# First layer of a graph network: one product of 144 columns per tile and bucket instead of three of 48, into three banks in turn

## What is computed

```
x = _layernorm(x + _L0_gnn_ref(x, edge_weight1, ..., src, dst, edge_type_8))    # relations
x = _layernorm(x + _L1_gnn_ref(x, edge_weight1, src, dst))                     # softmax over edges
x = _layernorm(x + _L2_gnn_ref(src, dst, x))                                   # two propagations
x = _layernorm(x + _L3_gnn_ref(x, edge_index, edge_attr_40, ...))              # gated messages
```

```
h1 = relu(einsum('ni,rij->nrj', inputs, weight1) + bias1)
h2 = einsum('nrj,rjo->nro', h1, weight2)
msg = h2[src, rel_type] * norm
agg = segment_sum(msg, dst, num_segments=6250)
return relu(agg + bias2)
```

## Time and profile before

| | us |
|---|---|
| runs shown, median of 3 | 6890.07 (6889.62 to 6891.36) |
| the profiled execution's own time | 6896.36 |
| its span | 6894.1 |
| first layer, first to last L2229 | 232.5 to 2764.1 |
| PE busy | 3935.5 (57%) |
| DVE busy | 4076.4 (59%) |
| POOL busy | 3949.5 (57%) |
| ACT busy | 2562.1 (37%) |

### The profile page before, as it was taken

The page is one execution under the profiler, slowest core; times in us unless marked ns, Lnnn a source line. Parts: engine busy times, 40 slices in busy tenths (PEclk is TensorE's granted clock), DMA queues, the critical chain, the costliest instruction groups (busy, mean ns, idle before and its releaser), DMA issues.

```text
span 6894.1 us, 121916 instructions
## 1 busy us (share of the span) xinstructions
PE 3935.5 (57%) x46612; PEld 3010.7 (44%) x46613; DVE 4076.4 (59%) x7184; ACT 2562.1 (37%) x5259; POOL 3949.5 (57%) x3993
## 2 busy tenths in 40 slices
PE   6455555545545554355555555556555565887775
PEld 5344444323323323134444444444444444776774
DVE  4444444555555556345566666566666568667999
ACT  1111111111111111244455445445445445776664
POOL 2566666666666666655555555555555553225996
PEclk8555555555555555555555555555555555999998
DMA  3455422222222222133333233333333332667886
GB/s 128 166 159 165 122 48 47 49 53 48 48 47 48 48 48 46 30 52 55 56 57 59 54 57 55 56 57 57 55 58 56 55 57 53 190 186 172 193 191 132
DMA packets 1414672, 571.31 MB, mean 83 GB/s; under 512 B 1069539, under 2 KB 1353711, under 8 KB 1413953
## 3 DMA queue, kind: packets, MB, share of 16 engines
q1 hardware_dynamic: 1309185, 452.39, 29.4%
q0 software_dynamic: 104896, 110.96, 7.3%
HBM read 394.81 MB, written 168.16 MB: 82 GB/s over the span
## 4 chain that ended last, share of the span: by engine, by line
another core or an unknown queue 23%; PE 18%; issue 16%; ACT 16%; DVE 13%; DMA 9%; SPq 2%; POOL 1%; DVEq 0%; ACTq 0%; POOLq 0%
DMA rb<-dst_rows 6%; PE ps L1250 4%; ACT rb L1606 3%; ACT meta_b L1616 3%; DMA meta_b<-blocks 3%; DVE ps L2099 2%; ACT meta_a L1538 2%; PE ps L1288 2%; PE ps L1421 2%; ACT rb L1636 2%; ACT at_table L1636 2%; PE ps L1210 2%; ACT meta_b L1623 1%; PE ps L1238 1%
## 5 line engine op out<-in xcount | busy, mean ns | idle before, releaser
L928 POOL DMA_INDIRECT by_src<-meta_a,row_src x1612 | 1609.5, 998 | 1343.2 <-DVE meta_a L2354 922.6
L917 POOL DMA_INDIRECT ring<-h_table,meta_b x1616 | 1641.9, 1016 | 945.8 <-issue 452.7
L1523 ACT ACTIVATE ring<-ring,meta_b 128x48 f32<-128x48 f32 x1616 | 386.4, 322 | 2142.1 <-DMA ring<-h_table,meta_b 2104.3
L1421 PE MATMUL ps<-dst_i,meta_b 128*128 128x128 bf16 x2450 | 398.7, 295 | 901.5 <-ACT rb L1636 331.5
L1250 PE MATMUL ps<-ring,WX 128*128 128x48 bf16 x2188 | 440.2, 235 | 559.7 <-DVE row_src L2230 331.3
L2593 DVE TENSOR_TENSOR meta_b<-big,ps 128x1152 bf16<-128x1152 bf16 x546 | 734.5, 1346 | 0.0
L1421 PEld LDWEIGHTS ps<-dst_i,meta_b 128*128 128x128 bf16 x2450 | 229.6, 152 | 1133.1 <-issue 1107.3
L1250 PE MATMUL ps<-row_src,WX 128*128 128x48 bf16 x4376 | 502.5, 233 | 261.5 <-issue 260.1
L1380 PE MATMUL ps<-WX,meta_b 128*128 128x49 bf16 (+1 forms) x14742 | 591.4, 200 | 61.0 <-issue 28.2
L1250 PEld LDWEIGHTS ps<-ring,WX 128*128 128x128 bf16 x2188 | 358.7, 164 | 591.7 <-DVE row_src L2230 343.3
L1288 PE MATMUL ps<-meta_a,w1T 40*48 40x256 f32 x806 | 401.6, 596 | 358.6 <-DMA meta_a<-in_attrT 179.1
(11 more groups left out here) (343 smaller groups left out, 9058.7 us busy)
## 6 DMA issues: line engine op xcount, KB each, us to landing
meta_b<-blocks SPq DMA_DIRECT2D x490, 144.0 KB
by_src<-default SPq DMA_DIRECT2D x44, 1456.0 KB
meta_a<-by_src SPq DMA_DIRECT2D x273, 216.0 KB, 4.4
rb<-lo_rows SPq DMA_DIRECT2D x202, 256.0 KB
rb<-src_rows SPq DMA_DIRECT2D x273, 144.0 KB
rb<-dst_rows SPq DMA_DIRECT2D x273, 144.0 KB
meta_a<-in_attrT SPq DMA_DIRECT2D x402, 80.0 KB
ring<-h_table,meta_b POOLq DMA_INDIRECT x1616
```

The lines of the kernel that those rows point to most:

```text
L917: pool.indirect_dma_start(ring[:, gg % RING, j, 0:width], None, table, bass.IndirectOffsetOnAxis(ap=index(g * GROUP + j), axis=0)) \
L928: pool.indirect_dma_start(by_src, bass.IndirectOffsetOnAxis(ap=row_src[:, t:t + 1], axis=0), rec[:, q % RECS, j, :], None).then_inc(s_sc[q ...
L1421: mm = pe.matmul(bank(5, P, at=i * P), ohS_n[:, a % 3, :, u * TRIO + i], ohK_n[:, a % 2, u * TRIO + i, :], start=True, stop=True)
L1523: scaled = act.activation(row, row, ACT.Copy, scale=meta_b[:, t, M_NORM:M_NORM + 1])
```

## The change

The upper half of the product still comes from ACT, but ACT now writes it to a buffer of two slots instead of back into the ring, and the three parts of a row lie there side by side, 144 columns. The buffer is the tensor `X`. So:

- `sum_fixed`: one product of 144 columns per tile and bucket, into bank `b % 3`; the three parts are not yet added to each other. The first product of a bucket starts the sum, so nothing is zeroed. Ahead of the first product of bucket b >= 3, PE waits until bucket b-3 has been taken out (`s_taken`).
- `take_bucket` on DVE: one reduction over the three parts, from PSUM to `V[:, b, :]`, in the iteration after the bucket's last group.
- ACT waits, from group 2 on, for PE's sums of group g-2 (`s_used`). POOL waits for ACT's copy (`s_rown`) in place of PE's sums.
- `relations` becomes one addition on `V` and is a step of `first_norm`, which starts at place 4 of the second stage (before: place 0); ACT's square root for it goes from place 7 to 12.
- `X` is loaded with `x` after the last sum. The tile numbers are loaded again for `cell_tables`, at group 12, into another tensor (`scratch`); `place_cells` uses another scratch tensor.
- For the form that isn't run, buckets are summed and taken out as before with one more step (`sums_out`, `late_sums`).

```diff
+FIRST_OF = [next(t for t in range(TILES_IN) if FROM[t] + WIDE[t] > b) for b in range(N_BUCKETS)]
+LAST_OF = [max(t for t in range(TILES_IN) if FROM[t] <= b) for b in range(N_BUCKETS)]
+ROLLS = 3
+assert all(FIRST_OF[b + ROLLS] // GROUP > LAST_OF[b] // GROUP + 1 for b in range(N_BUCKETS - ROLLS))
...
-        parts_w = row_src[:, 0:4 * GROUP * FEAT].bitcast(F32).rearrange("p (s i j w) -> p s i j w", s=2, i=2, j=GROUP)
-        parts_h = row_src[:, 0:4 * GROUP * FEAT].bitcast(BF16) \
-            .rearrange("p (s i j w k) -> p s i j w k", s=2, i=2, j=GROUP, k=2)[:, :, :, :, :, 1]
-        ring_h = ring[:, :, :, :].bitcast(BF16)[:, :, :, 1:2 * FEAT:2]
+        parts_x = X[:, :, :].rearrange("p b w -> p (b w)")[:, 0:2 * GROUP * PARTS * FEAT]
+        parts_w = parts_x.rearrange("p (s j i w) -> p s j i w", s=2, j=GROUP, i=PARTS)
+        parts_h = parts_x.bitcast(BF16).rearrange("p (s j c k) -> p s j c k", s=2, j=GROUP, k=2)[:, :, :, :, 1]
...
# SP
-                if g == PLAN_AT + 20:
-                    sp.wait_ge(s_hit2, 1)
-                    sp.dma_start(X[:, :, :], A["x"]).then_inc(s_node, 16)
+                if g == TILE_NO_AT:
+                    sp.dma_start(tile_at, A["tile_no"][:, 0:TILES_IN]).then_inc(s_node, 16)
+
+            sp.wait_ge(s_used, 2 * GROUPS_IN)
+            sp.dma_start(X[:, :, :], A["x"]).then_inc(s_node, 16)
...
# POOL, gather
-                    if gg >= RING:
-                        pool.wait_ge(s_used, 2 * (gg - RING + 1))
-                        pool.wait_ge(s_adapt, min(gg - RING + 1, GROUPS_IN))
+                    old = gg - RING
+                    if 0 <= old < GROUPS_IN:
+                        pool.wait_ge(s_rown, old + 1)
+                        pool.wait_ge(s_adapt, old + 1)
...
# PE, sum_fixed
                     for h in range(WIDE[T]):
-                        for rows in (ring_h[:, g % RING, j, :], parts_h[:, g % 2, 0, j, :], parts_h[:, g % 2, 1, j, :]):
-                            mm = pe.matmul(acc_of(FROM[T] + h, FEAT), hot_w[:, g % 2, h, :, j], rows,
-                                           start=False, stop=False, skip_group_check=True)
+                        b = FROM[T] + h
+                        if T == FIRST_OF[b] and b >= ROLLS:
+                            pe.wait_ge(s_taken, TAKEN + b - ROLLS + 1)
+                        mm = pe.matmul(bank(b % ROLLS, PARTS * FEAT), hot_w[:, g % 2, h, :, j], parts_h[:, g % 2, j, :],
+                                       start=(T == FIRST_OF[b]), stop=(T == LAST_OF[b]))
...
# ACT
+                if g >= 2:
+                    act.wait_ge(s_used, 2 * (g - 1))
...
-                    t, row = g * GROUP + j, ring[:, g % RING, j, 0:FEAT]
-                    scaled = act.activation(row, row, ACT.Copy, scale=meta_b[:, t, M_NORM:M_NORM + 1])
+                    t = g * GROUP + j
+                    scaled = act.activation(parts_w[:, g % 2, j, 0, :], ring[:, g % RING, j, 0:FEAT], ACT.Copy, scale=meta_b[:, t, M_NORM:M_NORM + 1])
...
# DVE, fixed_group
-                link(dve.tensor_tensor(rest, rows, ring_h[:, g % RING, 0:n, :], ALU.subtract))
-                dve.tensor_tensor(low, rest, parts_h[:, g % 2, 0, 0:n, :], ALU.subtract).then_inc(s_w, 2)
+                link(dve.tensor_tensor(rest, rows, top[0], ALU.subtract))
+                dve.tensor_tensor(low, rest, top[1], ALU.subtract).then_inc(s_w, 2)
...
+            def take_bucket(b):
+
+                dve.wait_ge(s_used, 2 * (LAST_OF[b] // GROUP + 1))
+                dve.tensor_reduce(V[:, b, :], bank(b % ROLLS, PARTS * FEAT).rearrange("p (i w) -> p w i", i=PARTS), AX_X, ALU.add) \
+                    .then_inc(s_taken, 1)
...
# DVE, end of an iteration of first_layer, and relations
+                    if fixed:
+                        for b in range(N_BUCKETS):
+                            if LAST_OF[b] // GROUP == g - 1:
+                                take_bucket(b)
...
             def relations():
-
-                for k in range(ACC_BANKS):
-                    last = dve.tensor_tensor(banks(V)[:, k], acc[:, k, :, 0:FEAT],
-                                             rb2[:, None, :].to_broadcast([P, PER_BANK, FEAT]), ALU.add)
-                last.then_inc(s_epi, 1)
-                dve.wait_ge(s_epi, 2)
+                return dve.tensor_tensor(V[:, :, :], V[:, :, :], rb2[:, None, :].to_broadcast([P, SLOTS, FEAT]), ALU.add)
```

More of the change, by code:

```diff
@@ L463, in build @@
         assert COS_AT < GROUPS_IN
-        NORM_AT = 7
+        FIRST_NORM_AT = 4
+        NORM_AT = FIRST_NORM_AT + 8
+        TILE_NO_AT = 12
         FIELDS_LAG, TABLES_LAG, ROWS_LAG = 10, 13, 16
@@ L1180, in sum_quads @@
                         for h, regs in enumerate((here, after)):
+                            rows = parts_w[:, gg % 2, t, 0, :] if gg < GROUPS_IN else ring[:, gg % RING, t, 0:width]
                             mm = pe.matmul(ps[:, bass.ds(regs[t], width)], W[:, i, j, h * P:(h + 1) * P],
-                                           ring[:, gg % RING, t, 0:width], start=False, stop=False,
+                                           rows, start=False, stop=False,
                                            skip_group_check=True)
@@ L2111, in _ @@
             rows_f = VQ[:, 2 * TILES_IN:3 * TILES_IN]
-            tmp = [VQ[:, i * TILES_IN:(i + 1) * TILES_IN] for i in range(2)]
+            tmp = big[:, TILES_IN:2 * TILES_IN]
             def place_cells():
@@ L2218, in fixed_group @@
             def fixed_group(g):
-                n, t = len(tiles_of(g)), g * GROUP
-                rows = ring[:, g % RING, 0:n, 0:FEAT]
-                rest, low = parts_w[:, g % 2, 0, 0:n, :], parts_w[:, g % 2, 1, 0:n, :]
+                n = len(tiles_of(g))
+                rows, rest, low = [parts_w[:, g % 2, 0:n, i, :] for i in range(PARTS)]
+                top = [parts_h[:, g % 2, 0:n, i * FEAT:(i + 1) * FEAT] for i in range(2)]
                 if g == 0:
@@ L2228, in fixed_group, with sums_out, first_layer @@
                     dve.wait_ge(s_used, 2 * (g - 1))
-                link(dve.tensor_tensor(rest, rows, ring_h[:, g % RING, 0:n, :], ALU.subtract))
-                dve.tensor_tensor(low, rest, parts_h[:, g % 2, 0, 0:n, :], ALU.subtract).then_inc(s_w, 2)
+                link(dve.tensor_tensor(rest, rows, top[0], ALU.subtract))
+                dve.tensor_tensor(low, rest, top[1], ALU.subtract).then_inc(s_w, 2)
                 if g + 1 < GROUPS_IN:
                     place_hots(g + 1)
-            def first_layer(weights_of):
+            def take_bucket(b):
+                dve.wait_ge(s_used, 2 * (LAST_OF[b] // GROUP + 1))
+                dve.tensor_reduce(V[:, b, :], bank(b % ROLLS, PARTS * FEAT).rearrange("p (i w) -> p w i", i=PARTS), AX_X, ALU.add) \
+                    .then_inc(s_taken, 1)
+            def sums_out():
+                dve.wait_ge(s_used, 2 * GROUPS_IN)
+                for k in range(ACC_BANKS):
+                    last = dve.tensor_copy(banks(V)[:, k], acc[:, k, :, 0:FEAT])
+                return last
+            def first_layer(weights_of, fixed):
                 early = [split(src_i, lo_src, link)]
@@ L2267, in first_layer @@
                         steps(early, 3)
+                    if fixed:
+                        for b in range(N_BUCKETS):
+                            if LAST_OF[b] // GROUP == g - 1:
+                                take_bucket(b)
                 steps(early, 1000)
+                if fixed:
+                    for b in range(N_BUCKETS):
+                        if LAST_OF[b] // GROUP == GROUPS_IN - 1:
+                            take_bucket(b)
+                    dve.memset(V[:, N_BUCKETS:SLOTS, :], 0.0).then_inc(s_epi, 1)
+                else:
+                    sums_out().then_inc(s_epi, 1)
             dve.tensor_copy(place_8, iota_b[:, 0:P][:, :, None].to_broadcast([P, P, GROUP])).then_inc(s_place, 1)
@@ L2288, in _, with late_sums @@
             dve.tensor_scalar(far[:, 1:2], small[:, 6, 0:1], 0.5, None, ALU.is_le).then_inc(s_far, 1)
-            def relations():
-                for k in range(ACC_BANKS):
-                    last = dve.tensor_tensor(banks(V)[:, k], acc[:, k, :, 0:FEAT],
-                                             rb2[:, None, :].to_broadcast([P, PER_BANK, FEAT]), ALU.add)
-                last.then_inc(s_epi, 1)
-                dve.wait_ge(s_epi, 2)
+            def late_sums():
+                for k in range(ACC_BANKS):
+                    last = dve.tensor_tensor(banks(V)[:, k], acc[:, k, :, 0:FEAT], banks(V)[:, k], ALU.add)
+                last.then_inc(s_epi, 1)
+                dve.wait_ge(s_epi, 3)
+            def relations():
+                return dve.tensor_tensor(V[:, :, :], V[:, :, :], rb2[:, None, :].to_broadcast([P, SLOTS, FEAT]), ALU.add)
             def cell_tables_of(d):
```

57 lines of the change are left out of this document (35 added, 22 removed).

## The result

| | before | changed |
|---|---|---|
| median of the runs beside each other, us | 6889.84 (4 runs, 6878.81 to 6891.36) | 6975.5 (4 runs, 6958.09 to 7000.69) |
| ratio, 95% interval | | 1.0133 (1.0108 to 1.0157) |
| span of the profiled execution | 6894.1 | 6969.6 |
| time of a group in the first layer | 12.59 | 13.01 |
| from the last group's subtraction to the end | 4130.0 | 4121.1 |

A forecast was written before the change was run, and what follows sets the result against it. The first layer was taken to be bound by the ring between DVE and PE, with POOL's gathers as floor. Terms -138 - 163 + 15 - 3 = -289 us gave 6607, with the runs' median 6601 us; range 6460 to 6790 (0.82).

The forecast's parts named there:

- the ring between DVE and PE: First layer: DVE splits, PE sums and counts, DVE scans before the next split; taken to set 12.59 us a group.
- The sums, -138: PE's sums: one product of 144 columns for three of 48, 187 to 124 ns at 2188 places, 138 us less.
- The back-to-back rule: PE's products follow each other by N / 1.2 ns at the low clock, which would make the sums' gain 0.
- The breaks, -163: Unexplained idle time before PE's sums, 488.0 us; middle between 325 us less and nothing taken, 163 us less.
- POOL's release: POOL's ring slot is free without PE's sums, so gathers may start earlier; data already wait for DVE, counted as nothing.
- ACT's copy, 0: ACT scales into two slots and waits for PE's group before the last; 18.7 us cover its 1.9, cost 0.
- the slower rival: ACT starts only at PE's late post and DVE's split waits: 384 us more, less the 289, about 6985 us; chance 0.07.
- The rest, -3: Five additions before the second stage become one inside it, 3 us less; moved load and late norm 0 each.
- breaks stay: Rival: PE's unexplained idle time does not shrink, only -138 + 15 - 3 = -126 us, 6764 us; chance 0.19.
- nothing moves: Rival: gathers pace PE by themselves, a group stays at 12.59 us whatever PE does, 6887 us; chance 0.07.

The follow-up runs named there:

- after_third: The changed kernel unaltered, run again on a chip where the kernel before takes 5611.4 us: 5606.1 us, ratio 0.9986.
- three_used: The changed kernel with three products of 48 columns and POOL again waiting for PE's sums: 6837.7 us, 1.0085 of the kernel before.
- used: The changed kernel with POOL's gather again waiting also for PE's sums of the slot's last group: 6811.0 us, 1.0031 of the kernel before.
- the holds: Kernels in which POOL's gathers of group g wait for PE's sums of g-3 or g-2; in the changed kernel 0.9858 and 0.9836 of the kernel before.
- The hold of g-2: The changed kernel with POOL's gather of group g waiting for PE's sums of g-2: 6771.64 us, 0.9836 of the kernel before.
- the two holds: The changed kernel, a group's first four gathers waiting for PE's sums of g-3, the last four for g-2: 0.9987 and 0.999; 0.9841 on a slower chip.

## Why the prediction was wrong

- *What bounds the kernel.* "POOL is not the bound" and "the ring between DVE and PE" were right by their rows and yet missed the point: on these chips the ring is long because POOL gathers. Halving the gathers took 4.9 us off the group with the ring's own work unchanged, 4.8 of them off DVE's wait for PE. I had written that I do not know what starves PE and that it decides the case; the sum then went on with a middle value.
- *The sums, -138.* The term was right in size. Eight products of 144 columns take 1.18 us, so (1.18 - 0.32) / 7 = 0.123 us each, where 0.124 was taken. PE's busy time from 200 to 1150 us fell from 462 to 369 us. As time it was worth 27 to 37 us under the old release. The back-to-back rule that I set against it ("TensorE: Matmul & The Clock Gate" of the Trainium skill, Back-to-back issue gap) gives 0.120 us for 144 columns, near the 0.123 measured; it is at 48 columns that the trace has 62 ns and the rule 40.
- *The breaks, -163.* This step failed. I took the middle between "goes with the count" and "goes with time", and it does not go with the count: 684.6 us of "issue" before PE's products became 634.1, and over all its products 753 became 779. It goes with the gathers (149 us with half of them) and with the chip (none before products in `after_third`). The statement that fetching is hidden ("Runtime: NRT & Kernel Launch" of the Trainium skill, Instruction fetch mechanics), which I had let speak for a rival only, fits this far: fewer instructions gave nothing of their own beyond the products' time.
- *POOL's release, "I count nothing".* This step failed too, and it is the largest cost: 0.7 to 1.0% with one product and 3.4% with three. I priced what the earlier start could bring, and not what the gathers that start earlier do to PE.
- *ACT's copy, 0.* This failed by size. DVE waited 15.0 us for it (10.8 before), so the slower rival that I had named (ACT as a link of the ring, 384 us) did not happen at its place. But ACT waits 2024 us for PE or "remote", and passes the lateness of PE's posts on to POOL, whose new release it is (243.8 us). Copy, wait and taking out together cost 46 to 58 us in `three_used`, of which I had 15, and 14 are the reductions. DVE's wait for ACT grew by 8 to 21 us; the rest, some 10 to 35 us, I cannot place. This cost and the product's gain nearly cancel, and with the release on top the sign turned.
- *The rest, -3.* It was -9.
- The forecast's sum was 289 us less, and the measured one is 86 more. Of the rivals, "breaks stay" had the breaks right, and "nothing moves" had PE paced by the gathers but not the loss; none had the release.

What stays open: why PE's posts are late while POOL gathers on some chips and not on others. The traces show the delay, that it goes with the number of gathers or of their rows, and that a post is prompt in a pause of POOL and mostly late outside one; they do not show the thing that is shared. Rows and gathers were not told apart. That the release costs is shown on one chip with three products, and with one product only across chips, as the change was not run beside `used`. How it costs is in part argued: DVE's wait for PE falls when the release is given back, with the holds and with half the gathers, but neither the mean lag of the sums' posts nor the share of double bursts, by which I meant to show it, orders the times. ACT's wait for PE was not taken out by itself. The hold of g-2 in the changed kernel was not run on a chip of 5610 us; the two holds were, at 0.999.

## What to carry to other kernels

If hand-overs between two engines are late while a third issues gathers, treat that third engine's start times as a cost: a wait that looks superfluous may be what keeps its work out of the way. Here a longer hold of the gathers made the change 1.6% faster than the kernel before, where with the earlier release it is 1.0 to 1.3% slower; where the kernel before takes 5610 us neither moved the time by over 0.15%. Idle time without a shown cause is not removed by removing instructions; find out first whether it goes with their number or with what other engines do meanwhile.

## What the runs showed of the hardware

- A semaphore post of PE came up to 10 us and more after its product had started (the lag's upper tenth is 8.9 us in the change, and 13 of the 188 groups whose event is on record have over 10) while gathers of POOL were being issued (pauses are 11% of these 13 lags), where the kernel before takes 6790 to 6890 us. Where it takes 5610 us the lag is 0.34 us in the same kernel.
- The same program took 5610 us in two batches of runs (chip numbers 9 and 7) and 6790 to 6890 in the others, with gathers (947 ns) and products of equal length. What the waits of this schedule are depends on the chip that a run falls on, and a ratio holds for its kind of chip: the change is 1.0133 and 1.0101 on two runs' chips and 0.9986 (0.9976 to 0.9996) on one of 5610 us.
- The granted clock stayed at its lower level, 1.2 GHz, through the layer in the changed kernel too, with PE's busy time from 200 to 1150 us down from 462 to 369 us (the columns are those of the earlier trace rows):

```profile
200.00:1150.00 950.00, 369.41 (x4431) 310.48 (x4431) 397.12 (x1036) 136.69 (x563) 599.74 (x576) 0.51 0.41 121
```
